# Layer-1 cross attention of a two-layer decoder: the probabilities become the stationary operand of the value products, the sums are transposed back, and the piece spacing is set anew

## What is computed

```python
x = _layernorm(x + _L0_attn_ref(x, ...))
x = _layernorm(x + _L0_xattn_ref(x, ctx_768, ctx_768, ...))
x = _layernorm(x + _L0_ffn_ref(x, ...))          # 32 experts of 64, gated, and a shared one
x = _layernorm(x + _L1_attn_ref(x, ...))
x = _layernorm(x + _L1_xattn_ref(x, ctx_768, mask_BxS2_bk0, ...))
x = _layernorm(x + _L1_ffn_ref(x, ...))

# _L1_xattn_ref, the part that changes: H = 12 heads of DH = 64, 1601 context tokens of 96 features
q = (query @ Wq.T + bq).reshape(b, tq, H, DH)
k = (cross @ Wk.T + bk).reshape(b, tc, H, DH)
v = (cross @ Wv.T + bv).reshape(b, tc, H, DH)
scores = jnp.einsum('bqhd,bkhd->bhqk', q, k) / jnp.sqrt(jnp.float32(DH))
scores = jnp.where(key_padding_mask[:, None, None, :], -jnp.inf, scores)
attn = jax.nn.softmax(scores, axis=-1)
out = jnp.einsum('bhqk,bkhd->bqhd', attn, v).reshape(b, tq, INNER)
return out @ Wo.T + bo
```

## Time and profile before

| | us |
|---|---|
| median of 3 runs | 2252.92 |
| lowest, highest | 2249.48, 2264.66 |
| the profiled execution | 2261.73 |
| its span, first to last instruction | 2259.7 |

### The profile page before, as it was taken

How to read it: one execution, slowest core, us unless ns; L and a number is a source line. 1 busy time by engine, 2 the same in 40 slices (tenths; PEclk the granted TensorE clock), 3 DMA queues, 4 the chain that set the end, 5 groups by cost and what they waited for, 6 DMA issues and landing times.

```text
span 2259.7 us, 41500 instructions
## 1 busy us (share of the span) xinstructions
PE 1937.0 (86%) x14968; PEld 1486.2 (66%) x14968; DVE 1385.3 (61%) x3712; ACT 869.3 (38%) x1779; POOL 977.8 (43%) x992
## 2 busy tenths in 40 slices
PE   6676889998798988889898888989889898989997
PEld 3444567667676667666676676766667666767885
DVE  5455557646776557755676557764677655774553
ACT  2422334334433344334343343433443334433443
POOL 2302353445335553345435363344533555335554
PEclk9677799989999989999999999999999999999998
DMA  5000000000000000000000000000000000000000
GB/s 165 25 0 1 3 23 1 1 1 25 3 1 1 1 26 3 1 2 3 25 2 1 1 26 3 1 1 3 25 3 1 1 1 1 3 1 1 1 1 6
DMA packets 24110, 22.69 MB, mean 10 GB/s; under 512 B 16266, under 2 KB 22132, under 8 KB 23412
## 3 DMA queue, kind: packets, MB, share of 16 engines
q1 hardware_dynamic: 23892, 19.89, 3.2%
HBM read 18.83 MB, written 1.05 MB: 9 GB/s over the span
## 4 chain that ended last, share of the span: by engine, by line
PE 39%; issue 25%; DVE 17%; POOL 15%; ACT 3%; POOLq 0%; DVEq 0%; ACTq 0%
POOL xp_l L1404 10%; POOL pr_l L1404 5%; PE ps L939 3%; PE ps L924 3%; PE ps L940 3%; PE ps L1088 3%; PE ps L941 3%; PE ps L926 3%; PE ps L925 3%; PE ps L895 2%; DVE xmax_x L1759 2%; DVE smax L1677 2%; PE ps L890 1%; PE ps L1073 1%; PE ps L1075 1%
## 5 line engine op out<-in xcount | busy, mean ns | idle before, releaser
L1404 POOL TENSOR_TENSOR xp_l<-xp 128x512 f16<-128x512 f32 (+1 forms) x672 | 668.2, 996 | 1029.0 <-ACT xp L1266 1028.4
L1266 ACT ACTIVATE xp<-ps 128x512 f32<-128x512 f32 (+1 forms) x672 | 377.2, 563 | 626.1 <-PE ps L926 625.6
L1759 DVE TENSOR_REDUCE xmax_x<-ps 128x1 f32<-128x512 f32 x576 | 394.8, 688 | 294.8 <-PE ps L895 277.9
L1404 POOL TENSOR_TENSOR pr_l<-pr 128x512 f16<-128x512 f32 (+1 forms) x248 | 250.4, 1030 | 216.8 <-ACT pr L1221 197.6
L939 PE MATMUL ps<-xp,c_tok 128*97 128x256 bf16 (+1 forms) x624 | 179.6, 288 | 8.2 <-ACT xo_x L1276 7.3
L939 PE MATMUL ps<-xp,cx_tok 128*97 128x256 bf16 (+1 forms) x624 | 177.2, 284 | 8.6 <-ACT xo_x L1276 7.6
L940 PE MATMUL ps<-xp,c_tok 128*97 128x256 bf16 (+1 forms) x624 | 177.9, 285 | 0.0
L924 PE MATMUL ps<-xq_h,c_hl 99*128 99x256 f16 (+1 forms) x624 | 175.9, 282 | 1.3 <-ACT xp L1266 1.3
L926 PE MATMUL ps<-xq_h,c_hl 96*128 96x256 f16 (+1 forms) x624 | 175.9, 282 | 0.0
L940 PE MATMUL ps<-xp,cx_tok 128*97 128x256 bf16 (+1 forms) x624 | 175.6, 281 | 0.0
L924 PE MATMUL ps<-xq_h,cx_hl 99*128 99x256 f16 (+1 forms) x624 | 174.7, 280 | 1.0 <-ACT xp L1266 0.9
(11 more groups left out here) (354 smaller groups left out, 4327.9 us busy)
## 6 DMA issues: line engine op xcount, KB each, us to landing
ct<-in_ctxT SPq DMA_DIRECT2D x8, 600.4 KB
raw_tok<-in_ctx SPq DMA_DIRECT2D x8, 576.0 KB
c_wg<-in_wg SPq DMA_DIRECT2D x1, 1088.0 KB, 7.7
c_wu<-in_wu SPq DMA_DIRECT2D x1, 1088.0 KB, 9.9
c_wd<-in_wd SPq DMA_DIRECT2D x1, 1088.0 KB, 5.1
xin<-in_x SPq DMA_DIRECT2D x8, 128.0 KB, 2.1
out<-ys SPq DMA_DIRECT2D x8, 128.0 KB, 1.9
c_wd<-in_sel SPq DMA_DIRECT2D x1, 768.0 KB
```

Source lines behind the costliest of these rows:

```text
L1266: fn(xp_slot(i, n)[0:k_, 0:w], bank(first_bank + n % 2, k_, 0, w), ACT.Exp, scale=scale).then_inc(xa_e[i].sem, 1)
L1404: sub = lambda out, a, b_: nc.gpsimd.tensor_tensor(out, a, b_, ALU.subtract)
L1759: red(cross.xmax[:, t, c:c + 1], bank(PART_BANK[q], P, 0, PARTS[c][1]), AX.X, ALU.max).then_inc(xa_xd[1].sem, 1)
```

## The change

1. **Values.** `values` takes the probabilities as the stationary operand (128 queries at a time, so two halves t of each tile) and the 97 columns of the context tile as the moving one. A full tile has 6 matmuls of 97 columns where it had 3 of 256. The sums stand in bank 3 as 128 queries by 2 x 97 columns.
2. **Sums and turn.** ACT's `gathered` copies bank 3 to a new tile `oq` (128 x 194 float32) at p = 1. PE's new `turn`, at p = 3 behind the scores, transposes the two halves into the unused half of that step's score bank. ACT's `turned` then copies them to `xo` (97 x 256) as before. The scores' semaphore of p = 3 is raised by the turn. A wait at p = 5 keeps the scores out of the bank until the copy is done. The last head of the last batch has a turn of its own (`last_turn`).
3. **Order of tiles.** The short tile is pair 3 (`SINGLE`), not pair 6, so that half a bank is free there; pairs 4 to 6 are full.
4. **Weights.** With the new weights `weave` puts 21, 13, 5, 26 and 19 stream steps into the five sublayers of a batch in the loop (before 21, 13, 4, 28, 18). Within the first self attention two late pieces now get two steps each.
5. **Memory.** The mask row uses the space of unused partitions of `ct32`, in place of a tile of its own. The transfers are the same in number, size and waits.

```diff
+SINGLE = 3
+CROSS_TILES = [[(NK - 1, LASTK)] if p == SINGLE else [(2 * (p - (p > SINGLE)) + j, P) for j in range(2)] for p in range(NPAIR)]
...
-        mrow_u8 = sb("mrow_u8", [P, CTX], U8)
+        mrow_u8 = ct32[:].bitcast(U8)[:, 0:CTX]
+        oq = sb("oq", [P, QT * (DC + 1)])
...
-        SELF = [[(1, 40), (1, 10), (2, 40), (1, 12), (2, 12), (3, 17), (3, 10), (1, 20), (2, 15), (1, 60), (1, 20), (3, 36), (3, 43), (1, 60), (2, 50), (1, 42), (4, 40), (0, 40)], [(1, 90), (1, 14), (2, 40), ...
+        SELF = [[(1, 40), (1, 4), (2, 40), (1, 12), (2, 15), (3, 17), (3, 10), (1, 20), (2, 15), (1, 60), (1, 56), (3, 36), (3, 43), (1, 60), (2, 125), (1, 54), (4, 40), (0, 48)], [(1, 90), (1, 14), (2, 36), ...
-        WEIGHT = [SELF[0], [... (1, 60), (1, 30), (7, 30), ...], [... (4, 47), (8, 40), (8, 40), (1, 54), (0, 47)], SELF[1], None, [(1, 21), (1, 15), (2, 30), (0, 30)]]
+        WEIGHT = [SELF[0], [... (1, 54), (1, 30), (7, 30), ...], [... (4, 42), (8, 40), (8, 40), (1, 54), (0, 28)], SELF[1], None, [(1, 52), (1, 15), (2, 24), (0, 27)]]
...
             def scores(b, h, p):
+                if p == SINGLE + 2 and h > 0:
+                    pe.wait_ge(xa_o[1].sem, xa_o[1].at(b, h))
...
-                m.then_inc(xa_s[1].sem, 1)
+                if p != SINGLE or h == 0 and b.known(0):
+                    m.then_inc(xa_s[1].sem, 1)

             def values(b, h, p):
                 pe.wait_ge(xa_l[1].sem, xa_l[1].at(b, n + 1))
                 if p == 0 and h > 0:
-                    pe.wait_ge(xa_o[1].sem, xa_o[1].at(b, h))
+                    pe.wait_ge(xa_oq[1].sem, xa_oq[1].at(b, h))
...
-                for j, (kt, k_) in enumerate(pair_tiles(p)):
-                    o = bank(3, DC + 1, 0, SEQ)
-                    mm(o, c.tok_h[0:k_, kt, :], xp_high(n, k_, j * SEQ, SEQ), start=(kt == 0), stop=False, skip_group_check=True)
-                    mm(o, c.tok_l[0:k_, kt, :], xp_high(n, k_, j * SEQ, SEQ), start=False, stop=False, skip_group_check=True)
-                    m = mm(o, c.tok_h[0:k_, kt, :], xp_l[0:k_, n % 3, j * SEQ:(j + 1) * SEQ], start=False, stop=(kt == NK - 1),
-                           skip_group_check=True)
+                ends = [p == 0, p == NPAIR - 1]
+                for j, (kt, k_) in enumerate(CROSS_TILES[p]):
+                    for t in range(QT):
+                        o, q0 = bank(3, P, t * (DC + 1), DC + 1), j * SEQ + t * P
+                        mm(o, xp_high(n, k_, q0, P), c.tok_h[0:k_, kt, :], start=ends[0] and j == 0 and t == 0, stop=False, skip_group_check=True)
+                        mm(o, xp_high(n, k_, q0, P), c.tok_l[0:k_, kt, :], start=False, stop=False, skip_group_check=True)
+                        m = mm(o, xp_l[0:k_, n % 3, q0:q0 + P], c.tok_h[0:k_, kt, :], start=False, stop=ends[1] and j == 1, skip_group_check=True)
...
+            def turn(b, h, n):
+
+                pe.wait_ge(xa_oq[1].sem, xa_oq[1].at(b, h + 1))
+                for t in range(QT):
+                    m = nc.tensor.transpose(bank(1 + n % 2, DC + 1, SEQ + t * P, P), oq[:, t * (DC + 1):(t + 1) * (DC + 1)], ident)
+                m.then_inc(xa_s[1].sem if n < TOTAL else last_turn.sem, 1)
...
                         scores(b, h, p)
+                        if p == SINGLE and h > 0:
+                            turn(b, h - 1, n)
...
+            def gathered(b, h):
+
+                act.wait_ge(xa_pv[1].sem, xa_pv[1].at(b, h + 1))
+                nc.scalar.copy(oq[:], bank(3, P, 0, QT * (DC + 1))).then_inc(xa_oq[1].sem, 1)
+
+            def turned(b, h, n):
+
                 if h > 0:
-                    act.wait_ge(xa_f[i].sem, xa_f[i].at(b, h))
...
+                    act.wait_ge(xa_f[1].sem, xa_f[1].at(b, h))
...
+                nc.scalar.copy(cross.xo[:], bank(1 + n % 2, DC + 1, SEQ, SEQ)).then_inc(xa_o[1].sem, 1)
```

More of the change, by code:

```diff
@@ L1033, in cross_steps @@
                         scores(b, h, p)
+                        if p == SINGLE and h > 0:
+                            turn(b, h - 1, n)
+                        elif p == SINGLE and not b.known(0):
+                            turn(b.plus(-1), XH - 1, n)
                         if joins and p == 4:
@@ L1050, in cross_end @@
                 values(b, XH - 1, NPAIR - 1)
+                turn(b, XH - 1, TOTAL)
                 yield
@@ L1263, in exps, with sums @@
                 act.wait_ge(xa_s[i].sem, xa_s[i].at(b, n + 1))
-                w, k_ = (2 * SEQ, P) if p < NPAIR - 1 else (SEQ, LASTK)
+                w, k_ = (2 * SEQ, P) if p != (NPAIR - 1, SINGLE)[i] else (SEQ, LASTK)
                 first_bank, scale = (6, 1.0) if i == 0 else (1, XD ** -0.5)
                 fn(xp_slot(i, n)[0:k_, 0:w], bank(first_bank + n % 2, k_, 0, w), ACT.Exp, scale=scale).then_inc(xa_e[i].sem, 1)
-            def sums(b, i, h):
-                act.wait_ge(xa_pv[i].sem, xa_pv[i].at(b, h + 1))
+            def sums(b):
+                act.wait_ge(xa_pv[0].sem, xa_pv[0].at(b, 1))
+                nc.scalar.copy(front.xo[:], bank(5, DC + 1, 0, SEQ)).then_inc(xa_o[0].sem, 1)
+            def gathered(b, h):
+                act.wait_ge(xa_pv[1].sem, xa_pv[1].at(b, h + 1))
+                nc.scalar.copy(oq[:], bank(3, P, 0, QT * (DC + 1))).then_inc(xa_oq[1].sem, 1)
+            def turned(b, h, n):
                 if h > 0:
-                    act.wait_ge(xa_f[i].sem, xa_f[i].at(b, h))
-                elif i == 1 and not b.known(0):
+                    act.wait_ge(xa_f[1].sem, xa_f[1].at(b, h))
+                elif not b.known(0):
                     act.wait_ge(xa_f[1].sem, xa_f[1].at(b.plus(-1), XH))
-                side, bk = (front, 5) if i == 0 else (cross, 3)
-                nc.scalar.copy(side.xo[:], bank(bk, DC + 1, 0, SEQ)).then_inc(xa_o[i].sem, 1)
+                nc.scalar.copy(cross.xo[:], bank(1 + n % 2, DC + 1, SEQ, SEQ)).then_inc(xa_o[1].sem, 1)
             def context_attention(b):
@@ L1329, in cross_steps @@
                         if p == 1 and h > 0:
-                            sums(b, 1, h - 1)
+                            gathered(b, h - 1)
                         elif p == 1 and not b.known(0):
-                            sums(b.plus(-1), 1, XH - 1)
+                            gathered(b.plus(-1), XH - 1)
+                        if p == SINGLE and h > 0:
+                            turned(b, h - 1, NPAIR * h + p)
+                        elif p == SINGLE and not b.known(0):
+                            turned(b.plus(-1), XH - 1, NPAIR * h + p)
                         if h == CUT and p == 4 and not b.known(NB - 1):
@@ L1337, in cross_end @@
             def cross_end(b):
-                sums(b, 1, XH - 1)
+                gathered(b, XH - 1)
+                act.wait_ge(last_turn.sem, 1)
+                turned(b, XH - 1, TOTAL)
                 yield
@@ L1466, in cross_steps @@
                 for n in range(h_from * NPAIR, h_to * NPAIR):
[L1468 removed]
+                    w, k_ = (2 * SEQ, P) if n % NPAIR != SINGLE else (SEQ, LASTK)
                     pool.wait_ge(xa_e[1].sem, xa_e[1].at(b, n + 1))
```

17 lines of the change are left out of this document (10 added, 7 removed).

## The result

| | before | after |
|---|---|---|
| median of 7 runs, us | 2252.45 | 2267.69 |
| lowest, highest | 2247.99, 2264.66 | 2261.35, 2274.58 |
| profiled execution, us | 2261.73 | 2274.58 |
| mean granted clock | 0.931 | 0.907 |

The ratio is 1.0071, with a 95% interval of 1.0045 to 1.0097: the changed kernel is 15 us slower. The forecast was 2198 us, in a range of 2174 to 2254. Time and sign were wrong.

A forecast was written before the change was run, and what follows sets the result against it. PE was taken as the bound, with gaps left by the front's chains. Tail 10.6, other heads 38.7 and weights 6 made 55 us off the profiled 2261.7; medians run 8.8 lower, so 2198 us, range 2174 to 2254.

The forecast's parts named there:

- Price of the value products: PE's value products: 78 matmuls of 97 columns at 44 ns, 3.43 us a head, 0.99 us less.
- Rivals A (strided load): Value products: strided loads set the pace, 60 ns for 52 of 78, about 2254 us, or 2239 at 56 ns; chance 0.13.
- C (54 ns or more): Value products: load and matmul pairs come no faster than in long runs, 57 to 60 ns, about 2292 us; chance 0.12.
- D (load not hidden): Value products: the load no longer hides behind so short a matmul, 104 or 58 ns each, 2514 us; chance 0.02.
- The turn: PE at p = 3: two float32 transposes cost 0.22 us a head, their delay of the exponentials hidden.
- It costs nothing with about 1 us to spare: ACT's turned copy before the output product of p = 4: 1.7 us of PE work covers 0.74 us of ACT.
- Order of the tiles at nothing: Short tile in step 3 instead of 6: same work in other places, zero cost, nothing pushed over two steps of lead.
- Weights: Stream steps moved beside idle PE time in the sublayers: 1 us a batch gained, 6 us over six batches.
- 0.62 of the saving kept outside the tail: 81 heads among fronts: 52 of 84 steps keep the 0.77 us saving, the rest precede waits; 38.7 us.
- rival B: Loop: PE's gain is lost in the waits of the front, only the tail gains, 2242 us; chance 0.12.
- the sign that it falls: Prediction falls if matmul starts are 54 ns apart or more, or idle PE grows as much as its work falls.
- Tail, 10.6 us: Tail's 15 heads, bound by PE, save 0.77 us each whole: 11.6 us, less 1 for the kernel's end.

The follow-up runs named there:

- e2: Kernel before with only the short tile moved from pair 6 to pair 3 of a head: 2299.02 us, ratio 1.0217.
- e5: Changed kernel with ACT's copy of the turned sums at p = 3 put ahead of the layer norm's piece: 2258.01 us, ratio 1.0009.
- e3: Changed kernel with the weights of before: 2290.65 us, ratio 1.0185.
- e8: Kernel before with the new weights only: 2269.05 us, ratio 1.0064.
- e1: Kernel before with six of the 39 value products of each head left out, nothing else moved: 2248.07 us, ratio 0.9971.
- e9: Kernel before with only one of the three value products of each tile: 2183.44 us, ratio 0.966.
- e14: Kernel before with DVE's row-maxima reductions halved to 256 columns and six value products a head left out: 2214.05 us, ratio 0.98.
- e6: Changed kernel with the short tile last, old weights, turn in bank 0 at step 3, ACT's copy ahead of the norm: 2253.76 us, ratio 1.0003.
- e7: Kernel before with five extra 512-column products on PE ahead of six long waits in each batch: 2270.55 us, ratio 1.0085.
- e10: Kernel before with seven more 256-column products a head, one for each pair, into unread columns: 2305.32 us, ratio 1.0208.

## Why the prediction was wrong, by its steps

The prices of the instructions were right; what failed is what they were worth in the loop, and one term that was put at nothing. Along the path of the experiments, the forecast had nothing for the order of tiles and 45 us were lost (e2). It had 49 us of gain for the swap, 10.6 in the tail and 38.7 outside it, and 8 came, not told from nothing. It had 6 for the weights, and 23 came. The three differences, 45 and 41 less 17, are the 70 us between the forecast and the result. The step that failed first is that PE's saving is kept at 0.62 outside the tail, the second that the order of equal work costs nothing.

- **Price of the value products**: right. 44 ns, forecast 44. Rivals A (strided load), C (54 ns or more) and D (load not hidden) are all refuted. The Trainium skill, "TensorE: Matmul & The Clock Gate", section "Weight-path perf modes — Fast Weight Load (FWL) and DoubleRow", says that the quick load takes strided columns too; the trace of after agrees, 97 ns for both. The section "Back-to-back issue gap" of the same page of the Trainium skill gives about 81 ns for such a pair at 128 columns. Before, with 57 ns at 128 columns, does not agree, nor does after fit it, with 44 ns at 97.
- **The turn**: right in price, 0.22 us. Work on PE fell by 69.6 us, forecast 74.
- **"It costs nothing with about 1 us to spare" (ACT's copy)**: wrong. The working looked at the tail, where ACT's queue holds the exponentials only. In the loop the copy came to stand behind a piece of the norm that waits for DVE, and PE waits for it up to 2.8 us once a batch. e5: 9.7 us. The instruction was priced and the queue it was put into was not read.
- **Order of the tiles at nothing**: wrong, the largest error of sign. e2: +45 us. The forecast asked what the short step's own wait would cost and not what a changed rhythm does to the fronts. The weights of before fit the old order (new ones gain 23 us on the new order and cost 15 on the old).
- **Weights**: forecast 6 us gained. On the new order they gain 23 (e3), on the old one they cost 15 (e8). Counting idle time in stretches gives neither.
- **0.62 of the saving kept outside the tail**: wrong. 38.7 us were forecast for 81 heads; e1 shows no gain in the six batches that hold 72 of them, for a cut of 0.68 us a head. The count of waits assumed that PE's saving is lost only in the step right ahead of a wait. e9 shows instead that PE's waits for DVE grow as PE's work shrinks. e14 shows that half-clock time does it as well, with DVE relieved. This is rival B, which had 0.12 and was read with the right evidence (DVE at 171 of 266.5 us, its reductions what PE waits for). Its time for the tail's gain alone, 2242 us, is near e1 (2248), which is the bare saving. It should have been the first theory. It too left out the order, and it looked for the loss in idle PE (42 us a batch; 36.5 were measured). In the batch shown, PE's idle time grew by as much as its busy time fell, 3 us, which the prediction names as the sign that it falls. B's price for the clock, 5 us a batch for a fall by 0.02, was about right: the clock fell by 0.024 and cost 41.6 us over the kernel.
- **Tail, 10.6 us**: too large. A head gained 0.3 us, not 0.77; e1, without the new order, gained 0.55 of 0.68, and e6, the swap in the old order, 0.5. PE busy for 11.47 of 11.60 us did not mean that nothing was close behind it.

What stays open: why PE is granted half clock more often with less work, as e1, e9 and e14 show in step with the size of the cut, and whether that is the cause of lost time or only the company of longer gaps. e5, where the time fell and the gaps did not, speaks for the cause; e7 speaks against a simple remedy. Also open is which chain carries the 45 us of e2, of which the larger part is half clock.

## What to carry to other kernels

An engine that is busy 86% of the span in a kernel with several interleaved chains is not proved to be the bound. Leave some of its work out, and some of its neighbour's, before building the change that saves it: here 64 us out of PE gave 6 us, and 144 out of DVE gave 53. When instructions are put into another engine's queue, look at every stretch in which that queue also holds a waiting piece of another chain, the loop's above all. Count what an experiment's edit takes out by the instructions of its trace before reading it: e1 took six products a head and not the seven it was planned for. A spacing fitted to a rhythm of steps must be priced together with that rhythm; the order of equal work alone moved this kernel by 2%.

## What the runs showed of the hardware

- A pair of load and matmul at 97 moving columns, with a fresh 128 x 128 stationary operand each, starts every 44 ns in runs of twelve; a stationary operand of every second 16-bit word loads in 97 ns, as a packed one does.
- The granted clock goes down with PE's work in kernels that differ by nothing else: half-clock time is 313 us at 1599 us of work, 389 at 1535, 647 at 1323, and with the reductions halved 293 at 1599 and 418 at 1534. Above the work of before it hardly changes (300 at 1651 in e7, 337 at 1671 in e10). The mean granted clock of all runs says the same: 0.910 to 0.919 in e1, 0.853 to 0.869 in e9, 0.920 to 0.941 in before.
- After a wait of 2.8 us PE ran for 6.8 us at half clock (granted clock 0.50, 1.2 GHz), as the stretch shown under e5.
